# The second layer's causal convolution moved from VectorE taps to tap-scaled projections on TensorE

## The reference

```
xn = layernorm(x);  h = rmsnorm(xn) * norm_w
u, z = split(h @ in_proj_w)                      # 128 -> 2 x 256 channels
u = silu(causal_conv(u, conv_w) + conv_b)        # 4 taps over time, per channel
dt, B, C from u @ x_proj_w;  dt = softplus(dt @ dt_proj_w + dt_proj_b)
state = exp(dt * A) * state + dt * B * u         # scan over 512 tokens, 256 x 16 states
y = (sum over 16 states of state * C + u * D) * silu(z)
x + xn + y @ out_proj_w + mixture_of_experts(xn) # top 2 of 8, and a shared one
```

## Time and profile before

| what | value |
| --- | --- |
| runs | 1457.02, 1466.71, 1463.31 us; median 1463.31 us |
| profiled execution | 1467.0 us, its span 1465.2 us |
| TensorE busy | 1113.0 us (76%), 3424 instructions |
| VectorE busy | 1122.3 us (77%), 1580 instructions |
| ScalarE busy | 652.6 us (45%) |
| GpSimd busy | 682.0 us (47%) |
| mean granted clock of TensorE | 0.877 |

### The profile page before, as it was taken

The page is one execution under the profiler, slowest core; times in us unless marked ns, Lnnn a source line. Parts: engine busy times, 40 slices in busy tenths (PEclk is TensorE's granted clock), DMA queues, the critical chain, the costliest instruction groups (busy, mean ns, idle before and its releaser), DMA issues. The chain is left out here.

```text
span 1465.2 us, 14015 instructions
## 1 busy us (share of the span) xinstructions
PE 1113.0 (76%) x3424; PEld 381.1 (26%) x3424; DVE 1122.3 (77%) x1580; ACT 652.6 (45%) x1016; POOL 682.0 (47%) x505
## 2 busy tenths in 40 slices
PE   4577878778755677877887876888787778777887
PEld 1122222222211222322232222223223222222222
DVE  3557777777633778887987988799788798989776
ACT  1111222122214556547555654655755565474543
POOL 0100111011100546655855865576586477558665
PEclk8568987888975789989999998999999899899999
DMA  5983466535100100010110100011010000101100
GB/s 145 259 187 82 113 144 137 124 90 124 29 28 19 41 13 21 22 29 17 22 31 23 22 16 22 16 29 29 16 22 23 24 19 17 29 16 22 29 1 8
DMA packets 52744, 75.38 MB, mean 51 GB/s; under 512 B 7687, under 2 KB 44488, under 8 KB 48064
## 3 DMA queue, kind: packets, MB, share of 16 engines
q1 hardware_dynamic: 52672, 74.64, 21.3%
HBM read 48.92 MB, written 6.82 MB: 38 GB/s over the span
## 5 line engine op out<-in xcount | busy, mean ns | idle before, releaser
L1078 POOL TENSOR_TENSOR hc<-hs,c_rep 128x512 f32<-128x512 f32 x256 | 350.0, 1368 | 320.2 <-DVE hs L1427 318.7
L1178 ACT ACTIVATE p_decay<-p_decay,a_neg 128x512 f32<-128x512 f32 x256 | 169.5, 662 | 320.5 <-PE p_decay L1578 320.2
L1427 DVE TENSOR_TENSOR_SCAN hs<-p_decay,dbu 128x512 f32<-128x512 f32 x256 | 309.7, 1210 | 0.0
L1421 DVE TENSOR_TENSOR dbu<-p_du,b_rep 128x512 f32<-128x512 f32 x256 | 175.5, 686 | 90.9 <-PE p_du L1583 86.6
L1578 PE MATMUL p_decay<-block_in,spread 96*128 96x512 bf16 x256 | 103.7, 405 | 157.9 <-DVE hs L1427 137.4
L1090 POOL TENSOR_TENSOR sg<-sg,g_in 128x512 f32<-128x512 f32 x144 | 205.5, 1427 | 11.5 <-ACT sg L1190 11.5
L1609 PE MATMUL p_u<-xw,w 128*128 128x512 f32 x288 | 177.2, 701 | 38.7 <-DVE xw L1411 37.4
L1598 PE MATMUL p_g<-y_xt,w 128*128 128x512 f32 x288 | 164.4, 654 | 0.0
L1616 PE MATMUL p_acc<-y_hid,w 128*128 128x512 f32 x288 | 160.6, 641 | 4.0 <-DVE y_hid L1440 4.0
L371 POOL TENSOR_TENSOR ex_rest<-ex,ex_part 128x1024 f32<-128x1024 f32 x8 | 17.0, 2128 | 276.5 <-ACT ex_part L422 276.5
L1440 DVE TENSOR_TENSOR y_hid<-p_u,sg 128x512 f32<-128x512 f32 x144 | 98.0, 681 | 58.1 <-issue 51.0
(11 more groups left out here) (163 smaller groups left out, 1578.0 us busy)
## 6 DMA issues: line engine op xcount, KB each, us to landing
qb<-rq_rows SPq DMA_DIRECT2D x32, 1024.0 KB, 13.9
block_in<-y_part SPq DMA_DIRECT2D x192, 64.0 KB, 2.0
stack<-ex_part SPq DMA_DIRECT2D x96, 64.0 KB, 2.1
w<-in_w SPq DMA_DIRECT2D x3, 1152.0 KB, 12.8
y_x<-layer_out SPq DMA_DIRECT2D x9, 256.0 KB, 2.8
x<-in_x SPq DMA_DIRECT2D x8, 256.0 KB, 3.1
rq_rows<-rq SPq DMA_DIRECT2D x8, 256.0 KB, 2.0
layer_out<-x SPq DMA_DIRECT2D x8, 256.0 KB, 2.4
```

The costliest lines, as they stand in the source:

```text
L1078: nc.gpsimd.tensor_tensor(hc[:, k % NA], hs[:, k % 4], c_rep[:, p], ALU.mult).then_inc(hc_done.sem, 1)
L1178: nc.scalar.activation(p_decay[:, k % ND], p_decay[:, k % ND], ACT.Exp, scale=a_neg[:, g:g + 1]).then_inc(da_done.sem, 1)
L1421: nc.vector.tensor_tensor(dbu[:, k % 4], p_du[:], b_rep[:, p], ALU.mult).then_inc(dbu_done.sem, 1)
L1427: nc.vector.tensor_tensor_scan(hs[:, k % 4], p_decay[:, k % ND], dbu[:, k % 4], 0.0, ALU.mult, ALU.add)\
```

## The change

The convolution and the projection are both linear, so they are made in one: conv(h @ W)[t, d] is the sum over k of h[t - 3 + k] @ (W * tap k)[:, d]. A new tile wtap holds the four weight matrices W times tap k. A DMA at the start of layer 1 brings the taps to all 128 partitions (4 x 256 numbers in each, 512 KB in all), and VectorE multiplies them by W, in one instruction of 1024 columns. ht gets three zero columns ahead of the tokens. `in_proj` for the two halves of u issues four products each instead of one, with the input shifted by k columns, summed in PSUM. ScalarE's copy into ur adds the bias, and Silu reads ur. `convolve`, its slots, and the semaphore conv_step are gone. ScalarE's first use of the shared conv tile in `dt_in` now waits for the last split of the batch before (part3).

```diff
-        ht = sb("y_ht", [128, T])
-        ur = sb("ur", [128, ST, CONV - 1 + T])
+        ht = sb("y_ht", [128, CONV - 1 + T])
+        wtap = sb("wtap", [128, CONV, DI])
+        ur = sb("ur", [128, ST, T])
...
+            sp.dma_start(wtap[:], io["taps"].unsqueeze(0).to_broadcast([128, CONV, DI])).then_inc(staged, 16)
             sp.wait_ge(stored0, 1)
...
             def silu_u_z(b, p):
+                act.wait_ge(prep_free.sem, prep_free.at(b, Z1))
                 for s in range(ST):
-                    act.wait_ge(conv_step.sem, conv_step.at(b, 4 * s + 4))
-                    nc.scalar.activation(u[:, p, s], conv[:, 1, s], ACT.Silu, bias=w["conv_b"][:, s:s + 1]).then_inc(u_done.sem, 1)
-                act.wait_ge(prep_free.sem, prep_free.at(b, Z1))
+                    nc.scalar.activation(u[:, p, s], ur[:, s], ACT.Silu).then_inc(u_done.sem, 1)
...
                 if s == 0:
-                    act.wait_ge(rest1.sem, rest1.at(b - 1))
+                    act.wait_ge(part3.sem, part3.at(b - 1))
...
                     if k == 1:
-                        copy_out(b + 1, HT, ht[:], scale=w["norm_w"])
+                        copy_out(b + 1, HT, ht[:, CONV - 1:], scale=w["norm_w"])
                     if k == 2:
-                        copy_out(b + 1, U0, ur[:, 0, CONV - 1:])
+                        copy_out(b + 1, U0, ur[:, 0], func=ACT.Identity, bias=w["conv_b"][:, 0:1])
                     if k == 3:
-                        copy_out(b + 1, U1, ur[:, 1, CONV - 1:])
+                        copy_out(b + 1, U1, ur[:, 1], func=ACT.Identity, bias=w["conv_b"][:, 1:2])
...
             dve.wait_ge(w_loaded, 16 * n_loads)
-            dve.wait_ge(staged, 32)
+            dve.wait_ge(staged, 48)
...
+            nc.vector.tensor_tensor(wtap[:], wtap[:], w["win"][:, 0:DI].unsqueeze(1).to_broadcast([128, CONV, DI]), ALU.mult).then_inc(tapped, 1)
...
-            def convolve(b, n):
-
-                s, k = divmod(n, CONV)
-                if k == 0:
-                    dve.wait_ge(prep_free.sem, prep_free.at(b, U0 + s))
-                    dve.wait_ge(part3.sem, part3.at(b - 1, s + 1))
-                taps = ur[:, s, k:k + T]
-                wk = w["conv_w"][:, s, k:k + 1]
-                if k == 0:
-                    ins = nc.vector.tensor_scalar(conv[:, 0, s], taps, wk, None, ALU.mult)
-                else:
-                    dve.wait_ge(conv_step.sem, conv_step.at(b, n))
-                    ins = nc.vector.scalar_tensor_tensor(conv[:, k % 2, s], taps, wk, conv[:, 1 - k % 2, s], ALU.mult, ALU.add)
-                ins.then_inc(conv_step.sem, 1)
...
-            conv_slot = {7: (0,), 8: (1,), 9: (2,), 10: (3,), 11: (4, 5), 12: (6, 7)}
...
+            pe.wait_ge(tapped, 1)
...
-                nc.tensor.matmul(p_misc[:], w["win"][:, bass.ts(n, 128)], ht[:], start=True, stop=True).then_inc(prep_full.sem, 1)
+                if n < ST:
+                    for k in range(CONV):
+                        ins = nc.tensor.matmul(p_misc[:], wtap[:, k, bass.ts(n, 128)], ht[:, k:k + T], start=(k == 0), stop=(k == CONV - 1))
+                else:
+                    ins = nc.tensor.matmul(p_misc[:], w["win"][:, bass.ts(n, 128)], ht[:, CONV - 1:], start=True, stop=True)
+                ins.then_inc(prep_full.sem, 1)
```

More of the change, by code:

```diff
@@ L901, in layer1 @@
         xw_done = count("xw_done", E + 1)
-        conv_step = count("conv_step", 2 * CONV)
+        tapped = outer.enter_context(nc.semaphore("tapped"))
         u_done = count("u_done", 2)
@@ L1048, in _ @@
             start(pool, [ln_rstd, xr_done, dt_step, hc_done, y_done, silu_done])
-            nc.gpsimd.memset(ur[:, :, 0:CONV - 1], 0.0).then_inc(begun, 1)
+            nc.gpsimd.memset(ht[:, 0:CONV - 1], 0.0).then_inc(begun, 1)
             pool.wait_ge(begun, 5)
@@ L1203, in prologue @@
                 copy_out(1, XT, xt[:, 0])
-                copy_out(1, HT, ht[:], scale=w["norm_w"])
-                copy_out(1, U0, ur[:, 0, CONV - 1:])
-                copy_out(1, U1, ur[:, 1, CONV - 1:])
+                copy_out(1, HT, ht[:, CONV - 1:], scale=w["norm_w"])
+                copy_out(1, U0, ur[:, 0], func=ACT.Identity, bias=w["conv_b"][:, 0:1])
+                copy_out(1, U1, ur[:, 1], func=ACT.Identity, bias=w["conv_b"][:, 1:2])
                 exp_gates(1)
@@ L1273, in _ @@
         def _(dve):
-            start(dve, [ln_stats, ln_var, ln_done, conv_step, sp_one, sp_step, rest1, part3, route, xw_done, dbu_done, scanned,
+            start(dve, [ln_stats, ln_var, ln_done, sp_one, sp_step, rest1, part3, route, xw_done, dbu_done, scanned,
                         y1_done, hid_done, res_done])
             dve.wait_ge(w_loaded, 16 * n_loads)
-            dve.wait_ge(staged, 32)
+            dve.wait_ge(staged, 48)
             nc.vector.tensor_copy(spread[:].rearrange("r i c -> r (i c)"), hs[0:96, 2]).then_inc(begun, 1)
@@ L1453, in prologue @@
                 normalize_rms(1)
-                for n in range(ST * CONV):
-                    convolve(1, n)
                 for n in range(15):
@@ L1491, in batch @@
                         continue
-                    if k in conv_slot:
-                        for n in conv_slot[k]:
-                            convolve(b + 1, n)
                     if 5 <= k < 20:
@@ L1728, in laid_out @@
                                   per_tile(a["L1_attn_dt_proj_b"]), per_tile(a["L1_attn_D"])], 1)),
+        "taps": c(a["L1_attn_conv_w"].T),
         "a_log": c(a["L1_attn_A_log"].reshape(GROUPS, 128 // N, N).transpose(1, 2, 0).reshape(128, GROUPS)),
```

## The result

| | before | changed |
|---|---|---|
| median of 20 runs each | 1461.24 us | 1468.91 us |
| lowest, highest | 1455.67, 1466.71 | 1457.70, 1483.15 |
| profiled execution, its span | 1467.0, 1465.2 | 1466.1, 1464.3 |
| granted clock, mean over the span | 0.877 | 0.901 |

The changed kernel takes 1.0047 times the time of the one before (95% interval 1.0026 to 1.0068), about 7.7 us more by the medians: slower by half a per cent, by the prediction's measure no change that counts. The ratio and its interval leave out the one slow run, the highest of the changed kernel (1483.15). The forecast was 1450, with faster as its sign. The time lies inside the range of 1432 to 1475, but the likeliest case did not happen. What happened is close to rival 2 (1473).

What follows compares the result with a forecast made beforehand. No engine is full; VectorE sets the time in steps 7 to 12, TensorE in steps 1 to 4. Prologue 10.2 + 7 x (4.5 - 7.8) = -12.9 us, giving 1450 us, own range 1442 to 1458, eight in ten 1432 to 1475.

Steps and rivals of the forecast that it cites:

- rival 2: Low clock stays at steps 10 to 12: 4.5 us goes and 4.5 comes per batch, prologue's 10.2 left; 1473, chance 0.24.
- Steps 11 and 12: Without taps, the hidden product's waits for TensorE mostly go if the clock stays high: 1.5 us more per batch.
- What goes: Convolution rows leaving VectorE: 7.1 us of path per batch, adjusted by step to 7.8 saved (4.5 with low clock).
- high-clock sum: VectorE's saving with TensorE's clock high: 7.1 - 1.0 + 0.5 - 0.35 + 1.5 = 7.8 us per batch.
- Net 0: ScalarE: copies add a bias, Silus lose theirs, as many instructions, no new table load; no time gained or lost.
- Steps 7 to 10: Without taps, step 8's wait passes to the ranking (1.0 back), step 9 gains 0.5 more, step 10 saves only 0.3.
- The products on TensorE: Six more float32 products per batch, in steps 2 and 3, cost 4.5 us; bounds 2.6 and 5.2.
- The signs named: New profile: steps 2 and 3 together 4 to 5 us longer, TensorE's rows back to back to step 4's decay product.
- The prologue: Layer 1's prologue and staging: products 7, later landing 1.9, tap multiplication 1.3; together 10.2 us more, bounds 6 and 16.
- Rival 1: Port waits for GpSimd in steps 7 to 9 go too: 2.5 us more saved per batch, 1433; chance 0.22.
- Rival 3: TensorE has room in steps 2 to 4, so products cost 2.6 instead of 4.5 per batch: 1437; chance 0.07.
- Rival 4: Waits of steps 11 and 12 go, but scans then wait for GpSimd's products: 2 us lost per batch, 1464; chance 0.05.

Runs made afterwards that it cites:

- Experiment 1: The kernel before with the convolution left out and Silu reading the projected u: 1428.04 us, ratio 0.9764.
- experiment 4: The changed kernel with two unread float32 products ahead of step 12's up product and two ahead of step 14's x projection: 1452.86 us, ratio 0.9935.
- experiment 3: The changed kernel with four tap products only in the prologue and the last tap's product alone in the batches: 1437.16 us, ratio 0.9822.
- experiment 2: The kernel before, convolution kept, with each half of u projected four times in the batches: 1495.08 us, ratio 1.0244.
- experiments 7 and 10: Changed kernel, taps loaded during layer 0 and multiplied on GpSimd: 7 also pairs tap products in steps 8 to 11, 1437.59 us; 10 alone, 1469.20 us.

## Why the prediction was right or wrong

- **The failed step is "Steps 11 and 12" of "What goes".** It counted on the 2.4 GHz level once the steps were shorter, put 1.5 us of gain there, and so chose 7.8 over 4.5 per batch. Experiment 1 measured 4.6, and in its trace the level of step 12 makes 1.7 us. The up pair of step 12 stayed at 1.2 GHz in five of the six middle batches, and the idle time ahead of it stayed too: 2.10 us before, 2.03 after. TensorE waits there for VectorE's product xw, and that stands behind the gates' row of 1.30 us, held up beside GpSimd's product. Over seven batches the 3.3 us between the two sums are 23 us too few, and the prologue was 4 us too many: together 19, the error (1450 against 1469). Where all the pairs were made fast by filling the gaps (experiment 4), the changed kernel came to 1453.
- **The high-clock sum itself was too large.** At the high level the convolution is worth 5.9 us (experiment 1, batches 3 and 5), 6.1 in batch 2 of the changed kernel, not 7.8. Two terms are missing in it: the port wait of step 11, and ScalarE's chain, which it put at nothing ("Net 0"). So the clock is only about half of what the 7.8 has too much.
- **A step was missing.** Rival 2 has the low clock end at step 12. In the trace step 12 does better than it says (1.14 us gained against 0.3), and step 14 loses 1.46. Of that some 0.8 is ScalarE's chain. The rest is the x projection and the up product on the path: slow in four and three of six batches now, the x projection in one before. The sum of both is near the rival's, its place is not, so that its 1473 came so near is partly luck: "it decides at steps 10 to 12" is half right.
- **Steps 7 to 10** came out as worked out: the ranking of step 8 took over the wait (1.08 us, 1.0 taken), that of step 9 came down by 0.53 (0.5 taken), step 10 gained 0.28 (0.3 taken). Step 11 gained 1.47; its hidden product no longer waits, but 1.12 us of port wait came in the gates' row, which no term had.
- **The products on TensorE** were right where they stand: 4.5 taken, 4.51 in the table, 4.5 and 5.0 per batch by medians (the 5.0 with a slower step 14). The signs named (rows back to back, steps 2 and 3 longer by 4 to 5 us) are there.
- **The prologue** was sized at 10.2 and shows 6.4. The landing (2.2, 1.9 taken) and the multiplication (1.0, 1.3 taken) were about right, the products gave 5.1 and not 7, and 1.7 us were won back by Silu's start, which the sum did not have. The second half of u already ran near the high level. By the medians (experiment 3 against 1) prologue and staging come to 9.1.
- **ScalarE** was put at nothing. Its own rows cost nothing more and Silu stayed in step 13, as said; but just because u does not come earlier, 0.8 us of what VectorE gains is lost in step 14.
- **Rival 1** (ports come free, 1433) fell: three rows still wait. Rival 3 fell with the 4.51. Rival 4 has the size (1464) by accident; the scans (line 1414) show no idle time of their own.
- **The chances.** Rival 2 had 0.24 and the forecast 0.42. The last batch, low in the same place with no taps at all, was the nearest row to the question. It was one draw, though: that step takes 5.02 and 5.03 us in the last batch of before and of the changed kernel, and 3.3 in the last batch of seven of the other eleven profiles, with its code unchanged. It spoke for even chances of the low level, not for certainty. The warning against idle gaps between bursts, from the Trainium skill ("TensorE: Matmul & The Clock Gate", the table on why this matters), pointed the right way; experiment 4 agrees with it.

## What to carry to other kernels

Taking work off one engine leaves the others' idle gaps where they were. Look at what TensorE's level is in those gaps, and which row behind them is on the path: a fall that was free beside a busy VectorE (step 12) costs when VectorE is early. Then ask what the early engine will wait for next: here ScalarE's chain to the x projection kept 0.8 us of the gain. Added products are priced by the idle time of the step they stand in, not by their length: the same six cost 4.5 us where TensorE set the time and 1.3 in pairs among VectorE's steps. And a wait at a shared port goes with its place, not with the instruction that showed it.

## What was not expected of the hardware

- Four products per batch that nobody reads made the changed kernel 16 us faster (1468.91 to 1452.86) and the kernel before 5 us slower (1461.29 to 1466.13).
- The same row behind the same idle gap ran at 2.4 GHz in batch 2 and at 1.2 in batch 4 of one execution. What decides between them stays open; no row shows it.
- Six more products per batch in steps 2 and 3, taps untouched, came with a slow x projection in step 14 in five of six batches, where one was slow before (experiment 2). The cause stays open.
- The changed kernel's 20 runs spread over 25 us (19 without the highest), the 20 of before over 11. A level that falls differently from batch to batch would do this, but each kernel has one trace, so it is argued and not shown.
- Moving the staging took 3.1 and 3.3 us off the prologue and nothing off two medians (experiments 7 and 10). Layer 0 ended at 418.1 to 426.1 us in the four profiles that have it moved, at 416.1 to 425.0 in the nine without; that is too wide to say whether its loads pay for it. Where the 3 us go stays open.
